# Selective-scan kernel: C rows loaded by four transfers, layer weights loaded once per layer, two ScalarE copies and the first products by B a slot sooner

## The reference, cut to what matters

```python
xn = rmsnorm(x, norm_w)
xp, z = split(xn @ Win)                      # 256 channels each
xc = silu(causal_depthwise_conv(xp, conv_w) + conv_b)
dt, B, C = split(xc @ Wx, [64, 64 + 16])     # 16 states
delta = softplus(dt @ Wdt + bdt)
h[t] = exp(delta[t] * A) * h[t-1] + (delta[t] * xc[t]) * B[t]   # per channel and state
y[t] = sum over states of h[t] * C[t]
x = x + ((y + xc * Dp) * silu(z)) @ Wblk
```

## Time and profile before

| | us |
|---|---|
| median of 3 runs | 2149.78 |
| lowest, highest | 2137.57, 2152.32 |
| profiled execution, its own time | 2157.49 |
| its span, first to last instruction | 2155.7 |
| steps: first C load of window 0 to that of window 30 | 76.13 to 1638.60 |

### The profile page before, as it was taken

The page is one execution under the profiler, slowest core; times in us unless marked ns, Lnnn a source line. Parts: engine busy times, 40 slices in busy tenths (PEclk is TensorE's granted clock), DMA queues, the critical chain, the costliest instruction groups (busy, mean ns, idle before and its releaser), DMA issues. The chain is left out here.

```text
span 2155.7 us, 30569 instructions
## 1 busy us (share of the span) xinstructions
PE 1863.9 (86%) x10816; PEld 1164.5 (54%) x10816; DVE 1809.7 (84%) x1728; ACT 1632.2 (76%) x2957; POOL 1418.2 (66%) x1364
## 2 busy tenths in 40 slices
PE   6688888888888888888888888888887799999998
PEld 2344444444444444444444444444444489999998
DVE  4798898999988888888888888888888987777775
ACT  4898988898988888888888888888888633333333
POOL 2688887888888888888888888888888700000000
PEclk9899999999999999999999999999999899999999
DMA  7333333333333433444344344433333200000000
GB/s 245 83 62 78 63 78 62 79 62 79 64 81 65 80 67 83 70 78 72 73 76 74 72 75 79 69 80 68 80 63 74 84 1 11 11 11 11 11 6 11
DMA packets 72871, 139.64 MB, mean 65 GB/s; under 512 B 13072, under 2 KB 31120, under 8 KB 68112
## 3 DMA queue, kind: packets, MB, share of 16 engines
q1 hardware_dynamic: 66320, 119.28, 27.7%
q10 hardware_dynamic: 6400, 18.42, 4.5%
HBM read 63.85 MB, written 7.74 MB: 33 GB/s over the span
## 5 line engine op out<-in xcount | busy, mean ns | idle before, releaser
L791 DVE TENSOR_TENSOR_SCAN scan<-decay,dbu_ps 128x1024 f32<-128x1024 f32 x512 | 1152.7, 2275 | 205.5 <-PE dbu_ps L1016 144.6
L455 POOL TENSOR_TENSOR scan<-scan,c_rep 128x1024 f32<-128x1024 f32 x255 | 692.3, 2715 | 209.3 <-ACT du_t L592 102.7
L539 ACT ACTIVATE decay<-d_rep,a_cur 128x510 f32<-128x510 f32 x1024 | 665.6, 710 | 164.3 <-DMA d_rep<-delta 90.8
L1016 PEld LDWEIGHTS dbu_ps<-ident,scan 128*128 128x128 f32 x4096 | 467.7, 144 | 484.8 <-DVE scan L791 232.2
L1016 PE MATMUL dbu_ps<-ident,scan 128*128 128x128 f32 x4096 | 563.4, 282 | 183.3 <-DVE scan L791 118.7
L449 POOL TENSOR_SCALAR scan<-du_t,b_t 128x256 f32<-128x256 f32 x896 | 529.9, 608 | 0.0
L607 ACT ACTIVATE scan<-du_t,b_t 128x256 f32<-128x256 f32 x1024 | 446.0, 495 | 2.6
L800 DVE TENSOR_TENSOR scan<-scan,c_rep 128x1024 f32<-128x1024 f32 x257 | 316.4, 1231 | 2.3 <-DMA c_rep<-c_rows 2.3
L730 ACT ACTIVATE decay<-dbu_ps 128x512 f32<-128x512 f32 x256 | 148.3, 598 | 203.3 <-PE dbu_ps L1215 183.1
L1029 PE MATMUL pre_ps<-xn,w_pre 128*128 128x512 f32 x512 | 275.7, 667 | 24.0 <-DMA w_pre<-prepared_weights 18.8
L1001 PE MATMUL y_ps<-scan,sel 128*32 128x512 f32 x2048 | 274.9, 609 | 0.0
(11 more groups left out here) (102 smaller groups left out, 1415.6 us busy)
## 6 DMA issues: line engine op xcount, KB each, us to landing
d_rep<-delta SPq DMA_DIRECT2D x496, 128.0 KB, 6.3
c_rep<-c_rows SPq DMA_DIRECT2D x32, 1024.0 KB
w_pre<-prepared_weights ACTq DMA_DIRECT2D x15, 866.0 KB, 18.5
prepared_weights<-scan SPq DMA_DIRECT2D x3, 1122.0 KB, 13.1
scan<-in_conv_w SPq DMA_DIRECT2D x4, 512.0 KB, 4.8
w_out<-prepared_weights SPq DMA_DIRECT2D x16, 128.0 KB, 15.3
x_in<-in_x_rows SPq DMA_DIRECT2D x8, 256.0 KB, 3.5
d_rep<-in_w ACTq DMA_DIRECT2D x2, 1024.0 KB, 6.7
```

The source lines that it names most:

```text
L455: nc.gpsimd.tensor_tensor(ring[slot % RING], ring[slot % RING], c_rep[par][:, slot // PRS, :].unsqueeze(1).broadcast_to([128, 2, TG]), ALU ...
L539: last = nc.scalar.activation(decay[slot % DEC][:, u, :, 1:], src[:, :, 1:], ACT.Exp, scale=a_cur[:, b, m:m + 1])
L791: nc.vector.tensor_tensor_scan(ring[slot % RING].rearrange("p u t -> p (u t)"), decay[slot % DEC].rearrange("p u a t -> p (u a t)"), dbu_p ...
L1016: last = nc.tensor.transpose(dbu_ps[slot % 2][:, u, 128 * j:128 * j + 128], dbu_t[m % 2][:, j, b, :, :].rearrange("p q c -> p (q c)"), ide ...
```

## The change

1. The load of C is four transfers of 32 partitions x 2048 columns instead of one of 4 x 32 x 2048; the waits for it count four times as far.
2. `w_pre` (both parts) and `w_out` are loaded at the first step of a layer alone: `w_pre` three times in place of 15, the skip part three in place of 15, `w_out` four in place of 16. In the windows without `w_out` SyncE no longer waits for `o_ready`. The store of layer 0's `w_pre` (994 KB at the start), which nobody reads any more, is gone.
3. On ScalarE `copy_out` stands at slot 10 in place of 11, `copy_dut` at 13 in place of 14, and the first products at slots 13, 14 and 15, so that none is left for slot 0 of the next window.

```diff
@@ -322,7 +322,6 @@
                              Wblk[l, :, :].rearrange("(k p) n -> p k n", k=KT)).then_inc(raw_loaded[l], 16)
             sp.dma_start(x[:, 2 * TG:], xT[:, 2 * TG:]).then_inc(x_ready, 16)
             sp.wait_ge(made_ready, 1)
-            sp.dma_start(w_dram[0, :, 0:W_PRE], w_pre).then_inc(made_stored[0], 16)
             sp.dma_start(w_dram[0, :, W_OUT:W_ALL], made[:, 0, W_OUT:W_ALL]).then_inc(made_stored[0], 16)
 
             def replicate(s, par):
@@ -351,21 +350,19 @@
                     for l in range(1, LAYERS):
                         sp.wait_ge(made_ready, l + 1)
                         sp.dma_start(w_dram[l, :, :], made[:, l, :]).then_inc(made_stored[l], 16)
-                    sp.wait_ge(made_stored[0], 2 * 16)
+                    sp.wait_ge(made_stored[0], 16)
                 if has(s, 1):
 
                     sp.wait_ge(c_stored, 16 * (s + 2))
                     rows = c_dram[nxt, :, :]
-                    sp.dma_start(merged(c_rep[nxt]),
-                                 bass.AP(tensor=rows.tensor, offset=rows.offset,
-                                         ap=[[M * TG, Q], [0, CH], [1, M * TG]]))\
-                        .then_inc(c_loaded[nxt], 16)
-                if has(s, 0) and par == 0:
+                    for q in range(Q):
+                        sp.dma_start(merged(c_rep[nxt])[CH * q:CH * q + CH, :],
+                                     bass.AP(tensor=rows.tensor, offset=rows.offset + q * M * TG,
+                                             ap=[[0, CH], [1, M * TG]])).then_inc(c_loaded[nxt], 16)
+                if has(s, 0) and s % GROUPS == 0:
                     wait(sp, o_ready, s)
                     sp.wait_ge(small_loaded, 16 * N_SMALL)
-                    layer = i // (GROUPS // 2)
-                    sp.dma_start(w_out[:, :], w_dram[bass.ds(layer, 1), :, W_OUT:W_ALL]
-                                 .rearrange("a p n -> (a p) n")).then_inc(w_out_ready, 16)
+                    sp.dma_start(w_out[:, :], w_dram[s // GROUPS, :, W_OUT:W_ALL]).then_inc(w_out_ready, 16)
                 if has(s, 1) and not has(s, 0):
 
                     sp.wait_ge(delta_ready, 1)
@@ -437,7 +434,7 @@
                         pool.wait_ge(dut_ready, 2 * (s + 1))
                         pool.wait_ge(bt_ready, s + 1)
                     if s == 0 and m < 2:
-                        pool.wait_ge(made_stored[m], 16 if m else 2 * 16)
+                        pool.wait_ge(made_stored[m], 16)
                 for q, j in itertools.product(range(first, last), range(POOL_J)):
                     dst = dbu_t[m % 2][:, j, :, q, :]
                     src = du_t[par][:, j, :].rearrange("p (b c) -> p b c", b=UNITS)
@@ -450,7 +447,7 @@
 
             def times_c(s, i, par, slot):
                 if slot == 1:
-                    pool.wait_ge(c_loaded[par], 16 * (i + 1))
+                    pool.wait_ge(c_loaded[par], 16 * Q * (i + 1))
                 pool.wait_ge(scan_done, SLOTS * s + slot + 1)
                 nc.gpsimd.tensor_tensor(ring[slot % RING], ring[slot % RING],
                                         c_rep[par][:, slot // PRS, :].unsqueeze(1).broadcast_to([128, 2, TG]),
...
@@ -614,16 +611,12 @@
                 nc.scalar.activation(x[:, group_cols(s + GROUPS)], bank[:, :], ACT.Copy)\
                     .then_inc(x_ready, 1)
 
-            def load_w_pre(i):
-
-                layer = (i + 1) // (GROUPS // 2)
-                act.dma_start(w_pre[:, 0:W_D], w_dram[bass.ds(layer, 1), :, 0:W_D]
-                              .rearrange("a p n -> (a p) n")).then_inc(w_pre_ready, 16)
-
-            def load_w_skip(i):
-                layer = (i + 1) // (GROUPS // 2)
-                act.dma_start(w_pre[:, W_D:W_PRE], w_dram[bass.ds(layer, 1), :, W_D:W_PRE]
-                              .rearrange("a p n -> (a p) n")).then_inc(w_skip_ready, 16)
+            def load_w_pre(layer):
+                act.wait_ge(made_stored[layer], 16)
+                act.dma_start(w_pre[:, 0:W_D], w_dram[layer, :, 0:W_D]).then_inc(w_pre_ready, 16)
+
+            def load_w_skip(layer):
+                act.dma_start(w_pre[:, W_D:W_PRE], w_dram[layer, :, W_D:W_PRE]).then_inc(w_skip_ready, 16)
 
             def window(s, i, par):
                 nxt = 1 - par
@@ -639,8 +632,6 @@
                     if has(s, 0):
                         exps(s, i, par, slot)
                     m, p = slot // PRS + 1, slot % PRS
-                    if has(s, 0) and slot == 0:
-                        outer(s, par, 0, FIRST[2], FIRST[3])
                     if has(s, 0) and m < M and p:
                         outer(s, par, m, SHARE[p - 1], SHARE[p])
                     if slot == 0 and has(s, 2):
@@ -653,25 +644,23 @@
                         root(s + 2)
                     if slot == 7 and has(s, 1):
                         softplus(s + 1)
-                        if par == 0 and has(s, 2):
+                        if has(s, 2) and (s + 2) % GROUPS == 0:
                             act.wait_ge(delta_ready, s + 2)
-                            if not has(s, -1):
-                                act.wait_ge(made_stored[0], 2 * 16)
-                            load_w_pre(i)
+                            load_w_pre((s + 2) // GROUPS)
                     if slot == 10 and has(s, 1):
                         copy_bt(s + 1, nxt)
-                    if slot == 11 and has(s, -1):
+                    if slot == 10 and has(s, -1):
                         if not has(s, 0):
                             relu(0, 0)
                             route(0)
                         copy_out(s - 1)
-                    if slot == 12 and par == 1 and has(s, 0) and has(s, 1):
+                    if slot == 12 and has(s, 0) and has(s, 1) and (s + 1) % GROUPS == 0:
                         act.wait_ge(skip_done, s + 1)
-                        load_w_skip(i)
-                    if slot == 14 and has(s, 1):
+                        load_w_skip((s + 1) // GROUPS)
+                    if slot == 13 and has(s, 1):
                         copy_dut(s + 1, nxt)
-                    if slot >= 14 and has(s, 1):
-                        outer(s + 1, nxt, 0, FIRST[slot - 14], FIRST[slot - 13])
+                    if slot >= 13 and has(s, 1):
+                        outer(s + 1, nxt, 0, FIRST[slot - 13], FIRST[slot - 12])
                     if is_last(s):
                         if slot == 4:
                             copy_x(0)
@@ -795,7 +784,7 @@
 
             def times_c(s, i, par, slot):
                 if slot == 0:
-                    dve.wait_ge(c_loaded[par], 16 * (i + 1))
+                    dve.wait_ge(c_loaded[par], 16 * Q * (i + 1))
                 dve.wait_ge(scan_done, SLOTS * s + slot + 1)
                 nc.vector.tensor_tensor(ring[slot % RING], ring[slot % RING],
                                         c_rep[par][:, slot // PRS, :].unsqueeze(1).broadcast_to([128, 2, TG]),
@@ -1074,8 +1063,8 @@
                     pe.wait_ge(dut_ready, 2 * STEPS)
                 if not has(s, 1):
                     pe.wait_ge(router, 2)
-                if par == 0:
-                    pe.wait_ge(w_out_ready, 16 * (i + 1))
+                if s % GROUPS == 0:
+                    pe.wait_ge(w_out_ready, 16 * (s // GROUPS + 1))
                 nc.tensor.matmul(bank[:, :], ident[:, :], x[:, group_cols(s + GROUPS)],
                                  start=True, stop=False)
                 for k in range(KT):
@@ -1111,8 +1100,8 @@
                 wait(pe, g_ready, 2 * s - 1 + k)
                 if s == 0:
                     pe.wait_ge(first_rep, Q)
-                if par == 0:
-                    wait(pe, w_skip_ready, 16 * i)
+                if s % GROUPS == 0:
+                    wait(pe, w_skip_ready, 16 * (s // GROUPS))
                 last = nc.tensor.matmul(y_ps[k][:, :], w_pre[:, W_D + 128 * k:W_D + 128 * k + 128],
                                         xc[par][:, k, :], start=True, stop=False, skip_group_check=True)
                 if k == KT - 1:
@@ -1157,8 +1146,8 @@
                     if slot == 12 and not has(s, 0) and has(s, 1):
                         replicate_first(2, Q)
                     if slot >= 14 and has(s, 0) and has(s, 2):
-                        if par == 0:
-                            pe.wait_ge(w_pre_ready, 16 * (i + 1))
+                        if (s + 2) % GROUPS == 0:
+                            pe.wait_ge(w_pre_ready, 16 * ((s + 2) // GROUPS))
                         project_conv(s + 2, 0, (slot - 14) * KC // 2, (slot - 13) * KC // 2)
                     if is_last(s):
                         if slot == 6:
```

More of the change, by code:

```diff
@@ L603, in outer @@
                     if s == 0 and m < 2:
-                        act.wait_ge(made_stored[m], 16 if m else 2 * 16)
+                        act.wait_ge(made_stored[m], 16)
                 for n in range(first, last):
```

## The result

The changed kernel takes 2012.7 us (median of 4 runs, 2010.1 to 2014.5) against 2147.2 us (2137.6 to 2152.3) for the kernel before on the same chip: ratio 0.938, interval 0.934 to 0.941. The profiled execution took 2014.5 us, its span is 2012.7.

The account below looks back on a forecast made before the run. Bound: a loop through several engines, none full, 52.08 us a step. 31 x (52.08 - 49.2) = 89, plus 6 at the start, minus 3 for the layers: 92 us, so 2058 us; range 2030 to 2105.

Parts of the forecast that it names:

- loop (A, B, C, D): One step as a chain through ScalarE, copy_dut, GpSimd and TensorE: 51.45 us before, 48.5 forecast at full clock.
- second path through the copies of delta: ScalarE's wait for delta copies before slot 0's decays, 2.83 us in window 17; forecast to go and not bind.
- A and B: ScalarE from its last silu of z to copy_dut, 28.27 us forecast to become 27.01; then copy_dut itself, 1.07.
- chain C: GpSimd's products from the end of copy_dut to TensorE's first turn of the next window: forecast to keep 10.64 us.
- The half clock: TensorE at 1.2 GHz behind its idle before the first turn: 0.7 us a step forecast saved, between 0 and 1.7.
- D without the half clock: TensorE from its first turn to the next sync point: 11.47 us before, 9.8 forecast at full clock.
- The start: Window 0, where ScalarE waited 12.53 us for copies behind C: 6 us forecast saved, between 0 and 12.
- The layer changes: Three windows that still load weights: delta copies up to 1 us too late, 3 us lost in all.
- C on four engines: Rival: splitting C does not spread it over more DMA engines; 50.0 us a step, 2089 us; chance 0.08.
- the giving back: Rival: GpSimd's product by C slows 0.7 us beside VectorE, clock falls as before; 50.9 a step, 2116 us; chance 0.12.
- the slower case: Rival: C fills all DMA engines for 16 us, delaying all delta copies; 53.6 us a step, 2197 us; chance 0.05.
- More gain, no low clock at all and a start that gives 12: Rival: TensorE's low clock vanishes everywhere and window 0 saves 12 us; below 2033 us; chance 0.04.

Follow-up runs that it names:

- c4_only: The kernel before with C loaded by four transfers and nothing else: ratio 0.979, 51.12 us a step.
- before_pool_first: The kernel before with only GpSimd's last product of the next window at slot 14, not 15: ratio 1.001, 51.91 us a step.
- late4: The changed kernel with two extra GpSimd instructions of 512 columns behind its wait for copy_dut: ratio 0.983, 51.23 us a step.
- late4_pe_busy: late4 with twelve more TensorE products, results unread, ahead of the first turn: ratio 0.962, 49.77 us a step.
- c4_pe_busy: c4_only with twelve more TensorE products, results unread, ahead of the first turn: ratio 0.964, 49.74 us a step.
- no_c4: The changed kernel without item 1, so C in one transfer again: ratio 0.988, 51.22 us a step.
- c4_pool_first: c4_only with GpSimd's last product of the next window at slot 14, not 15: ratio 0.930, 47.34 us a step.
- no_copies: The changed kernel without item 3, copies and products where they were: ratio 0.982, 51.15 us a step.
- late1: The changed kernel with one extra GpSimd instruction of 256 columns behind its wait for copy_dut: ratio 0.940, 48.01 us a step.
- late2: The changed kernel with two extra GpSimd instructions of 256 columns behind its wait for copy_dut: ratio 0.946, 48.35 us a step.

## Why the prediction was too small

- **What bounds the kernel**: right as a loop (A, B, C, D), and right that a second path through the copies of delta runs beside it. The runs show that either alone holds the step: taking one away gives 0.979 (c4_only) or 1.001 (before_pool_first).
- **C by four transfers**: right. 266 GB/s against four times 66 forecast; ScalarE's wait at slot 0 is gone, the four entries (1.70 us) cost nothing. Of the two sections of the Trainium skill's "DMA: Bandwidth & Descriptors" the one on the engine count (4 before, 16 after) agrees with these numbers; the rule that two transfers to disjoint partition halves are not worth it gives as its reason that both spray over all sixteen engines, and so does not carry over to a load whose outermost count is 4.
- **A and B**: 27.06 and 1.05 us, forecast 27.01 and 1.07.
- **The step that failed**: "What is late next is GpSimd itself: its chain C keeps 10.64 us." It measured 9.78. The difference stood in the earlier trace rows: two products took 1.90 us there, while two take 0.93 where VectorE makes no product by C. I took a duration that depended on its neighbour for a constant. Against these 0.97 us stands GpSimd's product by C at the head of the chain, 2.52 us for 2.36, which now meets VectorE's from 849.97 to 851.16; with 0.06 less in the other products that leaves the 0.86. late4 brought the 0.96 us back by delay alone. Since A to C moved forward against VectorE by 1.26 us, the products now end (860.46) before VectorE's begins (861.16).
- **The half clock**: put at 0.7 us a step, halfway to nearly never; measured none. Its full price was put at 1.7 us, late4_pe_busy shows 1.46 and c4_pe_busy 1.38. The wait ahead of the first turn fell to 0.50 us, not 1.3, because of the same 0.86 us. So both errors have one cause. 0.86 + 0.7 = 1.56 us, against 49.2 - 47.67 = 1.53.
- **D without the half clock** was 9.8 and measured 9.78.
- **The start**: 9.1 us instead of 6, between the ends 0 and 12. **The layer changes**: nothing, where 3 us were to be lost.
- **Weights once per layer**: forecast to turn even windows into odd ones, so as part of the 2.9 us a step. Alone it does so (51.26, and 51.45 was the odd window), but C by four transfers does it too, and the two don't add.
- **The rivals**: C on four engines, the giving back and the slower case did not come; of the giving back the meeting came, but with 0.16 us where 0.7 were feared, and without the clock. C on four engines was priced too low: no_c4 is that case, 51.22 us a step instead of 50.0. The price had ScalarE 0.8 us late for its silu; in the run TensorE stands 3.44 us ahead of z and makes it at half clock. "More gain, no low clock at all and a start that gives 12" named the right side and had the clock, but not the meeting; 0.04 was too little for a case in which one row of doubled time stood open.

In sizes: 31 x 1.5 = 47 for C and the clock, 3 for the start and 3 for the layers make 53; the gain in span is 143 against 92, the difference 51. The two ends of the range were not worked out alike: start and layer changes are 3 us in 2089 and 6 us in 2033, which alike would be 2036; the measured 2012.7 lies outside either way.

The Trainium skill's page "SBUF — State Buffer", in its section on two separate sides, says that GpSimd and a VectorE instruction with two SBUF inputs take one port pair in turn, each for a whole instruction. The trace agrees with it: in c4_only VectorE's product runs from 965.06 to 966.32, and GpSimd's two products, 0.47 us each elsewhere, end at 966.67, so that the second ends only 0.35 us behind VectorE's, having taken three times its 0.47. In c4_pool_first it goes both ways: VectorE's product at 853.59 takes 1.75 us instead of 1.19 and ends 1.08 us behind GpSimd's product by C (854.26), and GpSimd's 128x256 product at 854.21 takes 1.60 us instead of 0.63 and ends 0.47 us behind VectorE's (855.34). These rows fit one turn after the other; that it is a lock and not a slower pace for both was not tested apart.

## What to carry to other kernels

When a step is moved, look at which instructions of other engines will run beside it afterwards, and compare durations of one shape between places (here two products in 1.90 us or in 0.93) before taking one as fixed. Where two loops bind nearly alike, edits alone measure nothing or even a loss, and together much: cost them as a pair, and test the smallest pair (here four transfers and one number). And an idle stretch of TensorE has a second price in the clock behind it, which a little delay elsewhere can switch on or off.

## What the runs showed of the hardware that was not expected

- TensorE idle for 2.6 us ahead of the first turn, with the engine at 2.4 GHz until then, was followed by half clock (1.2 GHz), 92 us in some 27 steps, so 3.4 us in each (c4_only, late4, no_copies); idle for 0.50 us (the change), 0.87 (late1) or 1.22 us (late2) was not. In before_pool_first, 13 idle stretches of 1.9 to 2.1 us ahead of z had the longer matmuls of half clock behind them in 6 steps and not in 7. late2 has 48.35 us a step, and late4, with 0.44 us more of delay, 51.23.
- Two GpSimd products by B take 0.93 us alone and 1.90 beside VectorE's product by C of 1.26 us.
- A load that repeats rows and whose outermost count is 4 moved 66 GB/s, the same bytes in four transfers of 32 partitions 266.
